# Thirteen fp32 products of the identity on TensorE ahead of the first load's work, in a two-layer graph attention kernel

## The reference

```python
def _L0_gnn_ref(x, mask, Wv, bv, Wk, bk, Wq, bq, Wo, bo):
    v = relu(x @ Wv + bv); q = relu(x @ Wq + bq); k = relu(x @ Wk + bk)
    scores = einsum('bnh,bmh->bnm', q, k)
    att = softmax(scores * mask - NEG * (1.0 - mask), axis=2)
    out = einsum('bnm,bmh->bnh', att, v)
    return relu(out @ Wo + bo)

def _L1_gnn_ref(hidden, mask, W_w, W_b, a_w, a_b):
    h = einsum('bnd,ed->bne', hidden, W_w) + W_b
    e, f = h @ a_w[:D], h @ a_w[D:]
    u = mask * exp(e[:, :, None] + f[:, None, :] + a_b[0])
    a = u / sum(u, axis=2, keepdims=True)
    return einsum('bnm,bmd->bnd', a, h)

x = _layernorm(x + _L0_gnn_ref(x, adj, ...))
x = _layernorm(x + _L1_gnn_ref(x, adj, ...))
```

## Time and profile before

| | us |
|---|---|
| median of 3 runs | 442.85 |
| the three runs | 437.96, 442.85, 443.32 |
| the profiled execution, its own time | 437.73 |
| its span, first to last instruction | 436.0 |
| TensorE busy | 403.1 (92%) |
| VectorE, ScalarE, GpSimd busy | 325.7, 306.9, 260.6 |
| mean granted TensorE clock | 0.976 |

### The profile page before, as it was taken

How to read it: one execution, slowest core, us unless ns; L and a number is a source line. 1 busy time by engine, 2 the same in 40 slices (tenths; PEclk the granted TensorE clock), 3 DMA queues, 4 the chain that set the end, 5 groups by cost and what they waited for, 6 DMA issues and landing times.

```text
span 436.0 us, 8669 instructions
## 1 busy us (share of the span) xinstructions
PE 403.1 (92%) x2918; PEld 375.8 (86%) x2918; DVE 325.7 (75%) x929; ACT 306.9 (70%) x569; POOL 260.6 (60%) x223
## 2 busy tenths in 40 slices
PE   3989999999999999999999999999999999997740
PEld 2769998999999999999999999999999999996640
DVE  2377589767887978877887978877887979888631
ACT  3586768786878778686878778686878677775510
POOL 3763572556247772869447772869447752751955
PEclk9999999999999999999999999999999999999685
DMA  6573264647381737476383737476373737246521
GB/s 231 183 244 128 93 207 142 265 135 251 101 336 48 255 133 275 160 245 238 100 337 97 260 127 266 171 252 231 104 283 98 251 135 239 102 146 210 180 95 48
DMA packets 36684, 80.72 MB, mean 185 GB/s; under 512 B 2592, under 2 KB 19104, under 8 KB 36640
## 3 DMA queue, kind: packets, MB, share of 16 engines
q1 hardware_dynamic: 36352, 79.70, 53.7%
q10 hardware_dynamic: 288, 0.46, 0.3%
HBM read 75.96 MB, written 4.19 MB: 184 GB/s over the span
## 4 chain that ended last, share of the span: by engine, by line
PE 85%; POOL 5%; DVE 4%; DMA 2%; ACT 1%; issue 1%; POOLq 0%; DVEq 0%; ACTq 0%
PE m_ps L927 12%; PE pt_ps L876 12%; PE av_ps L888 7%; PE av_ps L890 7%; PE av_ps L889 7%; PE s_ps L823 7%; PE s_ps L825 6%; PE s_ps L824 6%; PE m_ps L825 6%; PE m_ps L824 6%; PE m_ps L823 6%; PE m_ps L905 2%; DMA adjt_in<-in_adj_t_dram 1%; DMA xt_in<-in_x_t_dram 1%; DVE prob L577 1%
## 5 line engine op out<-in xcount | busy, mean ns | idle before, releaser
L585 DVE TENSOR_TENSOR prob_tl<-pt_ps,prob_th 128x512 fp32r<-128x512 f32 x128 | 84.4, 682 | 24.5 <-ACT prob_th L416 24.4
L577 DVE CUSTOM_DVE_ANT_0 prob<-s_ps,penalty 128x1024 f32<-128x1024 f32 x64 | 78.0, 1219 | 24.0 <-PE s_ps L825 22.2
L416 ACT ACTIVATE prob_th<-pt_ps 128x512 fp32r<-128x512 f32 x128 | 73.0, 592 | 28.4 <-PE pt_ps L876 28.3
L369 ACT ACTIVATE adj_t<-adjt_in 128x1024 fp32r<-128x1024 f32 x64 | 67.1, 1056 | 25.1 <-PE m_ps L927 15.4
L408 ACT ACTIVATE prob<-prob,neg_max 128x1024 f32<-128x1024 f32 x64 | 73.8, 1153 | 10.9 <-DVE neg_max L577 10.6
L927 PE MATMUL m_ps<-g,adj_t 128*128 128x258 f32 x512 | 76.3, 295 | 4.5 <-DVE g L648 1.9
L876 PE MATMUL pt_ps<-ident,prob 128*128 128x128 f32 x512 | 73.7, 273 | 0.0
L888 PE MATMUL av_ps<-prob_th,vh 128*128 128x256 f32 x256 | 73.6, 287 | 0.0
L927 PEld LDWEIGHTS m_ps<-g,adj_t 128*128 128x128 f32 x512 | 67.3, 195 | 6.0 <-ACT adj_t L369 3.4
L890 PE MATMUL av_ps<-prob_th,vl 128*128 128x256 f32 x256 | 72.4, 283 | 0.0
L889 PE MATMUL av_ps<-prob_tl,vh 128*128 128x256 f32 x256 | 72.4, 283 | 0.0
(11 more groups left out here) (99 smaller groups left out, 879.0 us busy)
## 6 DMA issues: line engine op xcount, KB each, us to landing
adj_in<-in_adj_dram SPq DMA_DIRECT2D x64, 512.0 KB, 4.3
adjt_in<-in_adj_t_dram SPq DMA_DIRECT2D x64, 512.0 KB, 4.2
xt_in<-in_x_t_dram SPq DMA_DIRECT2D x8, 512.0 KB, 6.8
x_in<-in_x_dram SPq DMA_DIRECT2D x8, 512.0 KB, 4.7
out_dram<-out_sb SPq DMA_DIRECT2D x16, 256.0 KB, 4.5
wb<-in_pack_b_dram ACTq DMA_DIRECT2D x1, 320.0 KB, 6.3
wa<-in_pack_a_dram ACTq DMA_DIRECT2D x1, 132.0 KB, 4.5
```

What stands on the lines that cost most here:

```text
L416: sc.activation(prob_th[n % 2][:, tiles(k), (i % 2) * P:(i % 2 + 1) * P], pt_ps[k][:, :].rearrange("p (c n) -> p c n", n=P), ACT.Copy).the ...
L577: v.tensor_tensor_reduce(out=prob[i % 2][:, :], in0=s_ps[:, :, :].rearrange("p a n -> p (a n)"), in1=penalty[:, n % RING, :], scale=-1.0, ...
L585: v.tensor_tensor(prob_tl[n % 2][at], pt_ps[k][:, :].rearrange("p (c n) -> p c n", n=P), prob_th[n % 2][at].bitcast(F32), ALU.subtract).th ...
```

## The change

A function `warm_up` is added to TensorE's list and called once, ahead of all passes. It waits until the identity is written and then multiplies the identity with itself 13 times, in plain fp32, into columns 0 to 127 of the bank pt_ps0. Each product starts and ends its own sum. Nothing reads the result, and no semaphore is raised.

```diff
+    WARM = 13
...
+            def warm_up():
+
+                pe.wait_ge(ident_ok, 2)
+                for _ in range(WARM):
+                    pe.matmul(pt_ps[0][:, 0:P], ident[:, :], ident[:, :], start=True, stop=True)
...
+            warm_up()
             for p in PASSES:
                 batch_pass(p)
                 if p == PASSES[0]:
```

## The result

The changed kernel takes 436.4 us in the median of 22 runs (434.5 to 441.55), the kernel before 439.06 in 22 runs of the same chips (436.3 to 443.32). The ratio is 0.9939, with a 95% interval from 0.991 to 0.9969: faster by 0.6%, or 2.7 us. The forecast for the change was -2.4 us. The forecast for the time, 440.4, is 4 us too high, because it was hung on a median of three runs that 22 runs didn't bear out. The profiled execution went from a span of 436.0 to 433.8.

The account below looks back on a forecast made before the run. TensorE, busy 92% of the span, was taken to bound the kernel, so only the head could gain. Products cost 0, the earlier clock gives -2.4: 442.85 - 2.4 = 440.4 us, range 434.9 to 443.4.

Parts of the forecast that it names:

- The cost of the products: Head of TensorE: thirteen products at 0.43 us each fit idle time from 1.5 to 7.1 us, cost 0 (bound 0.6).
- The clock: Head of TensorE: full clock by the first real product at 7.35 us instead of about 15.9; forecast chance 0.52.
- Rival 1: Head: the thirteen products don't move the clock, so the time stays 442.85 us; chance 0.20.
- the rule that spoke against it: Trainium skill: transposes against an identity don't count for the clock; if it covered these products, 0 instead of -2.4 us.
- The chain in the head: Head, from q and k through GpSimd's last kl to the scores of tile 0: -2.4 us, range 0 to 2.7.
- The wait for w_l laid bare: Head, before v of half 0: TensorE idles about 0.1 us at 9.2 for VectorE's w_l of the second pack.
- The way to the end: Behind the head: TensorE's queue is full, so time saved before it reaches the end one for one.
- The level: Whole kernel: 442.85 us, median of three times before, as the base from which 2.4 was taken.
- Rival 3: Head: slow executions are those with a much later clock rise; the change removes that too, giving 435.5 us; chance 0.15.
- Rival 2: Head: the clock falls again in a 1.9 us hole before 14.5 us; 1.2 us slower, 444.0; chance 0.10.
- Rival 4: Head: the thirteen products run late, to 21 us, delaying the real ones; 454 us; chance 0.03.

Follow-up runs that it names:

- filled holes: The changed kernel plus 5 identity products behind q of half 1 and 7 behind the transposes of tile 0: ratio 0.9954, median 437.16 us.

## Why the prediction was right, and where it was not

**The cost of the products** was right: from 1.41 to 7.0 (1.5 to 7.1 forecast), no delay, 0.27 us to spare.

**The clock** was right: up before the first real product. Four products don't do it, thirteen do. Rival 1, that the identity's products don't count, fell, and so did the rule that spoke against it, even for the fp32 transposes.

**The chain in the head** was right in its sum and wrong in one link. The text had k of half 0 wait for the second half of xtl and start at 8.47. It waits for the first half alone (its wait is for a count of one) and started at 8.05. So its eviction began at 9.00 and not 9.4, GpSimd was done with kl of half 0 before the next kh came (0.18 us of waiting at 13.00), and the last kl ended at 14.27 and not 14.5. The gain there is 2.6 where 2.4 was forecast. The wait for w_l laid bare was 0.28 us instead of 0.1, for the same reason. The later steps (eviction at 11.57 for 11.5, first maximum at 16.16 for 16.3) held.

**The way to the end** was right in the main: of 2.61 us at TensorE's full stretch 2.2 are left in the span, as the last aggregations wait for adj_t. The ratio of the runs says 2.7, with an interval from 1.4 to 4.0; the lower groups say 1.8 to 2.0. The forecast of 2.4 has one execution before in it, with the rise at 15.9 us. In another without a warm-up it came at 12.2, and there the full stretch began 0.6 us earlier.

**The level** was wrong. I took 442.85, the median of three, two of which lay in the upper group; with 122 runs a third do. The term -2.4 from the true median 439.06 would have given 436.7. The range from 434.9 to 443.4 holds the measured 436.4, but it also holds 439.06, the time of no change at all, and so the time alone tests little. What bears the forecast out is the head, link by link, and the ratio.

**Rival 3** was right that the spread is the clock's in part, and wrong on the place. What the slow profiles show isn't a late rise in the head but a fall behind the second hole (1.4 us), an early fall in the drain (about 1.2) and the 2.1 us for which VectorE is held there. They are of other kernels (four products, transposes, filled holes); no slow execution of the kernel before or of the changed kernel was profiled. The change removes none of the three. **Rival 2** saw the fall in a hole, but named the first (12.8 to 14.3 us), where no profile shows one, and took it for a cost of the change, while the kernel before has the second hole as well, and an upper group. **Rival 4** didn't come up: a plain fp32 product takes 0.43 us, as form_w1 said.

## What to carry to other kernels

An idle TensorE ahead of the first load is worth filling with products that nobody reads, up to the moment when the first real one can start and not beyond: four did nothing, thirteen gave 2 us, and of twenty-six the part that ran over (2.2 us) was paid for in full. Look for the second hole as well, the first bubble behind the warm-up, where the clock can fall again; with it filled, behind the thirteen products, no run of 45 was in the upper group, though the drain has its part in that group. And before you shorten a chain in the drain, look for an instruction whose time has two values: here 0.04 us in the order of two engines decided over 2.1. After ordering the two, look at what the longer one runs into next.

## What the runs showed of the hardware

The profile's granted clock reads 1.00 in the head where the pitch of 512-column matmuls is 0.43 us (kernel before, 8 to 10 us); only the pitch shows the lower level (1.2 GHz) there:

```profile
8.00:10.00 2.00, 2.00 (x6) 1.00 0.28 76
```

The rise came at 12.2, 15.9 and 16.3 us in three executions without a warm-up, and at 10.7 in one with four products. Transposes of an fp32 identity raised the clock as products do. Behind a hole of 1.8 us the clock fell in two profiles of nine and stayed down for about 3.4 us. A VectorE subtraction of 8 columns took 0.16 us alone and 2.26 when a GpSimd addition was under way; one on 8 columns with a single input (a tensor and a constant) took 0.17 alone and 0.94 to 1.23 beside the same addition.
